# A graph convolution with experts: two further matmuls on constants after each gathered chunk's product

## The reference, cut to what matters

```
def gcn_conv(x, W, b, src, dst, n_nodes):
    loop = jnp.arange(n_nodes)
    s = jnp.concatenate([src, loop])
    d = jnp.concatenate([dst, loop])
    ...
    msg = xw[s] * norm[:, None]
    out = jax.ops.segment_sum(msg, d, num_segments=n_nodes)
    return out + b
...
out = gcn_conv(x, W1, b1, src, dst, N_NODES)
out = jax.nn.relu(batch_norm(out, gamma1, beta1))
out = gcn_conv(out, W2, b2, src, dst, N_NODES)
```

## Time and profile before

| | |
|---|---|
| median of three runs | 6377.77 us |
| the profiled execution | 6376.87 us, span 6375.1 us |
| mean granted TensorE clock | 0.716 |
| TensorE busy, matmuls | 4356.3 us |
| GpSimd busy | 3431.6 us |
| the gathers, L610 | 3328 of 946 ns |
| the products, L1612 | 6656 records of 539 ns |

### The profile page before, as it was taken

One profiled execution on the slowest core, in us unless ns is written; L12 is line 12 of the kernel. 1 busy time (PEld: TensorE's weight loads), 2 busy tenths in 40 slices (PEclk: granted clock), 3 DMA queues, 4 the chain that ended last, 5 costly groups with the idle time before them and its releaser, 6 DMA issues. The chain is left out here.

```text
span 6375.1 us, 79641 instructions
## 1 busy us (share of the span) xinstructions
PE 4356.3 (68%) x15178; PEld 2151.3 (34%) x15179; DVE 1894.7 (30%) x6972; ACT 1191.2 (19%) x2762; POOL 3431.6 (54%) x3661
## 2 busy tenths in 40 slices
PE   4566766666666767656666666667666665559999
PEld 4322222222222222232222222222222223448888
DVE  7311111212121111251112211211212216656665
ACT  5100000000000000120000000000000005535554
POOL 0466666666666666566666666666666661321111
PEclk5667676776766666766776667666776766679999
DMA  4633333333333333243333333333333332321111
GB/s 115 203 107 88 88 90 88 88 89 87 89 88 89 90 88 87 76 125 89 88 88 88 89 88 89 89 88 89 88 88 87 89 87 69 108 74 48 50 49 45
DMA packets 261857, 564.42 MB, mean 89 GB/s; under 512 B 67263, under 2 KB 136225, under 8 KB 261794
## 3 DMA queue, kind: packets, MB, share of 16 engines
q0 software_dynamic: 171264, 466.46, 25.3%
q1 hardware_dynamic: 90530, 97.27, 5.4%
HBM read 503.39 MB, written 60.09 MB: 88 GB/s over the span
## 5 line engine op out<-in xcount | busy, mean ns | idle before, releaser
L610 POOL DMA_INDIRECT ring<-messages,idx_stage x3328 | 3147.7, 946 | 1878.6 <-issue 875.7
L1612 PE MATMUL ps<-ring,onehot_mem 128*64 128x256 f32 x6656 | 2758.9, 539 | 1272.3 <-DMA ring<-messages,idx_stage 611.4
L1612 PEld LDWEIGHTS ps<-ring,onehot_mem 128*64 128x64 f32 x6656 | 952.1, 179 | 2731.9 <-DMA ring<-messages,idx_stage 1564.5
L1105 DVE TENSOR_TENSOR acc<-acc,ps 128x128 f32 x832 | 239.8, 288 | 3763.1 <-remote 1985.4
L744 ACT ACTIVATE win_rows<-ps 64x256 f32<-64x256 f32 x832 | 312.6, 377 | 2172.7 <-PE ps L1612 1120.9
L1094 DVE TENSOR_SCALAR onehot_mem<-iota_bf,tables 128x64 f32<-128x64 bf16 x3344 | 645.2, 266 | 232.4 <-issue 164.5
L1510 PE MATMUL ps<-ident,win_rows 64*128 64x64 f32 x1664 | 335.2, 293 | 404.8 <-ACT win_rows L744 319.6
L733 ACT ACTIVATE idx_stage<-tables 128x8 int32 (+1 forms) x420 | 87.1, 208 | 2371.5 <-PE ps L1612 1010.6
L1510 PEld LDWEIGHTS ps<-ident,win_rows 64*128 64x128 f32 x1664 | 204.8, 172 | 900.8 <-issue 900.8
L1817 PE MATMUL ps<-acc 128*128 128x256 f32 x2048 | 466.6, 380 | 0.8 <-ACT acc L907 0.8
L669 POOL DMA_INDIRECT out_dram<-acc x128 | 128.3, 1002 | 599.1 <-DVE acc L1463 415.4
(11 more groups left out here) (249 smaller groups left out, 2159.0 us busy)
## 6 DMA issues: line engine op xcount, KB each, us to landing
ring<-messages,idx_stage POOLq DMA_INDIRECT x3328
rows_mem<-in_x_dram SPq DMA_DIRECT2D x54, 448.0 KB, 4.2
acc<-routed_rows SPq DMA_DIRECT2D x64, 264.0 KB
messages<-dinvT SPq DMA_DIRECT2D x23, 448.0 KB, 6.2
dinvT<-in_x_dram SPq DMA_DIRECT2D x22, 448.0 KB, 4.0
messages<-ring SPq DMA_DIRECT2D x19, 448.0 KB, 3.2
dinvT<-dinv_row SPq DMA_DIRECT2D x28, 224.0 KB
messages<-rows_mem SPq DMA_DIRECT2D x14, 448.0 KB, 3.2
```

Of the source, the lines that this page charges most:

```text
L610: pool.indirect_dma_start(out=slots[:, s, :], out_offset=None, in_=t_dram[layer], in_offset=bass.IndirectOffsetOnAxis(ap=idx_stage[:, u, s ...
L1105: dve.tensor_tensor(sums(w, WIN), sums(w, WIN), ps[:, 2 + u, 0:KH * WIN].rearrange("p (k w) -> p k w", k=KH), ALU.add).then_inc(ev_fast, 1)
L1612: pe.matmul(ps[0:WIN, u, 0:D], onehot[:, u, j, 0:WIN], slots[:, s, :], start=j == 0, stop=j == CPG - 1).then_inc(chunks_used, 1)
```

## The change

Behind each product of a gathered chunk TensorE does two more matmuls. Both take as weights the first 64 columns of `iota_bf` and as moving data all 256 columns of it twice (512 columns, bf16), and write 64 x 512 values to PSUM banks 6 and 7. Nobody reads them. They carry no wait and no report of their own; the product's report to `chunks_used` stays on the product, ahead of them.

```diff
+                def stay_busy():
+
+                    for r in range(2):
+                        pe.matmul(ps[0:WIN, 6 + r, :].rearrange("p (r w) -> p r w", r=2), iota_bf[:, 0:WIN],
+                                  iota_bf[:, :].unsqueeze(1).to_broadcast([P, 2, GWIN]), start=True, stop=True)
+
                 def fast(i, q):
                     g, u = i * 4 + q, q % 2
                     pe.wait_ge(oh_fast, g + 1 + run * (NG + 2))
...
                         pe.matmul(ps[0:WIN, u, 0:D], onehot[:, u, j, 0:WIN], slots[:, s, :],
                                   start=j == 0, stop=j == CPG - 1).then_inc(chunks_used, 1)
+                        stay_busy()
                     if not isinstance(g, int) or g > 0:
                         turn_window(g - 1, 1 - u)
```

## The result

The changed kernel took 6447.19 us (6438.85 to 6458.75) against 6376.83 us beside it: a ratio of 1.0117, 95% interval 1.0103 to 1.0130. It is 70 us slower; forecast were 185 us.

A forecast was written before the change was run, and what follows sets the result against it. The prediction took TensorE's late reports, which make GpSimd stand in the gather stages, as the bound. To 6377 us it added 185 us for more frequent stands, other stages unchanged: 6562 us, range 6250 to 6830 us.

The forecast's parts named there:

- What bounds the kernel: Gather stages: gathers start every 1.25 us, but GpSimd stands because TensorE's reports come late, not from TensorE's speed.
- 774: Time in us that the two gather stages take beyond 4160 us, put down to GpSimd's stands, 3.6 us every 15.5 gathers.
- When the delay begins: While gathers run, TensorE's reports fall behind after some 50 of its instruction records, until a stand of GpSimd clears them.
- The cost of one matmul: Each added 512-column matmul on TensorE takes 0.41 us at half clock, 0.20 us at full clock.
- The clock: TensorE's granted clock in the gather stages rises to 0.85 to 0.95 instead of 0.69.
- No wait is added: The added matmuls wait for nothing; the window's turn behind them comes 0.4 to 0.8 us later, hidden by early masks.
- Records: Gather stages: 36 records a group, not 20, bring a stand every 12.7 gathers; 0.055 us a gather, +185 us.
- the clock pays: Rival, faster, chance 0.24: stands come from half-clock groups, so a steady 2.4 GHz cuts them; 6120 to 6250 us.
- The change doesn't hold the clock: Rival, slower, chance 0.14: TensorE still falls to half clock, where a group needs 7.4 us; 6560 to 6940 us.
- Clock regained, nothing else: Rival, no change, chance 0.12: gathers set the 1.483 us mean, stands come as often as before; 6364 to 6390 us.
- What would show it: Signs: clock 0.85 or more, runs of 11 to 13 gathers, copies 4 to 8 us late, TensorE busy over 80%.

The follow-up runs named there:

- four_short_g: Four added matmuls of 8 columns per product in place of the change's two of 512, with late reports: 6453.93 us beside 6311.55 for the kernel before, 1.0220.
- after_again: The changed kernel measured again, in a set with late reports: 6388.23 us beside 6315.33 for the kernel before, 1.0114.
- before_again: The kernel before, unchanged, measured again for its trace in a set with late reports: 6313.88 us.
- one_long: One added matmul of 512 columns per product in place of the change's two, without late reports: 5564.49 us beside 5568.25 for the kernel before, 0.9994.
- two_short_b: Two added matmuls of 8 columns per product in place of the change's two of 512, in a set without late reports: 5558.88 us.
- two_short_f: Two added matmuls of 8 columns per product in place of the change's two of 512, with late reports: 6446.75 us beside 6364.18 for the kernel before, 1.0128.

## Why the prediction was half right

*What bounds the kernel* held: gathers 1.25 us apart with stands between, and stands that follow TensorE's late reports and not its speed. The sets without late reports show it. There the kernel before, at the same mean granted clock (0.70 to 0.72 in either condition), needs 5559 to 5568 us. The prediction gave the two stages 4160 us without stands; the traces of the variants without late reports have 4160 to 4172 us from the first to the last gather of the layers. 6377 - 774 = 5603 us is 35 to 44 us more than was measured for the whole kernel, since late reports also cost some 48 us behind the gather stages.

*When the delay begins* held in part. The short matmuls show that instructions matter and array time doesn't. But there is no fixed point of "some 50 records" after a stand. Counted over all runs of gathers of a trace, from the first gather after a stand to the end of the first group that is copied over 1.5 us late, where there is one, TensorE leaves 44 and 50 records in the two traces of the kernel before (medians), 67 in the changed kernel and 71 in `four_short_g`. The time until then falls, 12.2, 9.0 and 6.5 us: the delay does begin earlier, but after more records.

*The cost of one matmul* held at full clock: 0.20 us were forecast, and eight of them with four products and the turn took 3.86 us where 4.1 us were written. The 0.41 us at half clock I did not read from a trace by itself. *The clock* held: 0.85 to 0.95 forecast, 0.91 and 0.90 measured. *No wait is added* held: the added matmuls (L1609) had 0.6 us of idle time before them in 1000 us.

*The size was wrong*, in the step *Records*: "then a stand of 3.6 us falls on" 12.7 gathers in place of 15.5, with the length of a stand kept as it was. The stands did become more frequent, 337 for 266 or 1.27 times, about what 15.5 / 12.7 = 1.22 says. But each became shorter, 2.41 for 2.83 us, and the sum grew by 59 us, 8%, where the forecast had it grow by 185 us, 24%. In the forecast's own terms: 2.83 us on 12.5 gathers became 2.41 us on 9.9, 0.018 us a gather and not 0.055. With the old length 71 more stands would have cost 201 us; that they are shorter took 142 us back. The same was seen in another set, 2.33 for 2.58 us (`after_again`, `before_again`), and 2.24 us with 32 added records is the shortest. For 8 records, 2.54 us, it isn't shown, since the same kernel's stands differ by as much from set to set. Why a stand shortens is not shown; that a shorter run leaves less behind to clear is my reading of it. The 3.6 us was also too long for today's stand: it put all of the 774 us on a stand at every 15.5 gathers, and the count gives 2.83 us at every 12.5. And 0.055 us was a choice between 0 and 0.095, not a price; 3.6 us on 12.7 gathers is 0.051 us a gather, or some 170 us and not 185.

*The rivals:* "the clock pays" fell: no run at a higher clock was faster than its kernel before beyond the interval; 0.9994 (0.9985 to 1.0003) for `one_long` is the nearest. Its argument against, that the two matmuls take what the clock gives, wasn't even needed: where the clock alone could have acted, without late reports, nothing waits for TensorE. "The change doesn't hold the clock" fell with 0.91. "Clock regained, nothing else" is what happened in the sets without late reports, for a reason that the prediction hadn't: I had not asked whether the late reports belong to the kernel at all.

*What would show it:* runs of 11 to 13 gathers in place of 15 or 16 were forecast, the median went from 13 to 10; TensorE's busy share over 80%, measured 79%; copies 4 to 8 us behind, 5.9 us in the group shown, but a median of 2.3 us and a ninetieth percentile of 6.7 us over all groups (before: 2.3 and 7.3). The prediction also says that a stand clears the reports and that both copies it shows came when GpSimd stood; the one at 2038.01 came while gathers were still 1.25 us apart. Of the copies over 2 us late 64% fall into a stand before the change and 77% after it.

The Trainium skill (NOTIFIC — the notification-queue block, section 7.1 Overflow) says that the block's internal pipeline holds up its producer rather than lose a record inside the block. That the loss follows the number of records and not the array time agrees with it. Over two thirds of the semaphore records of the gather stages are missing from the late traces all the same; no row says where they are lost, inside that block or elsewhere. No run here shows the block, and none shows what brings the condition on, so this stays open.

## What to carry to other kernels

A throttled clock in the profile is worth nothing by itself: first ask who waits for the engine's speed, here nobody in either condition. When a wait names an engine whose instruction had ended long before, compare its end with the first instruction elsewhere that uses it; if reports are late, extra instructions on that engine cost even when they are short, 5 to 7 ns a record here. Deepening one buffer can move the wait to the next, so look who waits afterwards. And run the kernel before at several times and on several chips before a stall is taken for a property of the kernel: the 1.2% of this change, and the 13% between the conditions, depend on something that no kernel here set, and that may belong to the recording.

## What the runs showed of the hardware

The same program took 5559 to 5568 us or 6312 to 6377 us, 13 to 15% apart, two of the chips showing both at different times. Between `two_short_b` and `two_short_f`, one program on one chip, the spans differ by 889 us: 838 us in the two gather stages and 48 us between the last gather and the end, in the router's stage with its indirect DMAs (L653). In the gather stages reports of TensorE's matmuls arrive late, up to 10 us with eight slots and 19 us with sixteen, while indirect gathers run 1.25 us apart, and most of the late ones come in when the gathers pause (64% before the change, 77% after it). The mean granted clock of the kernel before is the same in both, 0.70 to 0.72. In the last stage, with 9.5 TensorE records a us and without such gathers, the time is the same before and after the change. Not settled is what brings the condition on. No kernel of these runs switched it on or off; that is why the comparison within one set is the only one that counts here.
